# Graph layer and LSTM on one core: recurrent weights rounded in the graph's tail, low parts in 16 pieces, another order in the block loop

## The chip, the cores and the metric

The kernel runs on one core of one Trainium2 chip. The metric is the device time of one execution in microseconds. Three executions of the kernel before took 2735.42, 2737.44 and 2739.93 us; the median is 2737.44 us.

## The reference

A layer norm of x (6250 nodes, 512 features), a graph layer over 100000 edges sorted by destination, then a second layer norm and an LSTM over the 6250 rows as one sequence, each with a residual:

```python
agg = segment_sum(x[src], dst, 6250)            # x is the normalised input
h = relu((x + agg) @ W1 + b1)
x = x_in + relu(h @ W2 + b2)
# LSTM over the rows of layernorm(x), hidden size 512, f32
f, i, o = sigmoid([x_t, h] @ W_{f,i,o} + b); g = tanh([x_t, h] @ W_c + b_c)
c = f * c + i * g;  h = o * tanh(c);  y_t = x_t_in + h
```

## The kernel before

It has three stages with a barrier between them, each with a program of its own per engine and semaphores between these. Products are made in a rounded f32 type: each operand is split into a high part (rounded by ScalarE, `ACT.Copy`) and a low part (what is left, a subtraction), and two or three products are added.

**Table stage** (`table_part`, 0 to about 198 us). The rows of x are normalised and multiplied by W1; the result goes to DRAM as `ln_table`. GpSimd makes the low parts of W2 and of the LSTM's input weights here (L335, L339).

**Graph stage** (`graph_part`, to about 1402 us). 50 blocks of 125 nodes. Each block has 16 columns of 128 edges, and 7 blocks have one surplus column more. For each column GpSimd issues an indirect gather of 128 rows of 2 KB (L801) into a ring of 16 row buffers; it waits until VectorE has made the low part of the column that used the buffer before. ScalarE makes the high part (L836, 8 buffers), VectorE the low part (L994) and, four columns at a time, the one-hot matrix of destinations (L986); TensorE adds one-hot x high and one-hot x low to `agg` (L884). A surplus column is read after the 16 of its block: GpSimd waits for both consumers, loads the edges, waits for them, and gathers.

The loop is a software pipeline written out by hand: iteration i gathers block i, runs the layers of block i-1 and makes the LSTM's input products (`gps`, 48 matmuls, L904) of blocks i-1 and i-2. TensorE's order: turn `hin` (L898), columns 0 to 4, second layer `late` (12 products, L930 and L934), columns 5 to 7, gate products of banks 3 and 2, column 8, low gate products, columns 9 and 10, low products, turn z, columns 11 to 14, gate products, column 15, gate products. ScalarE's order: high parts 0 to 4, first layer (`first_layer`: relu of the turned rows, L848, and their high part, L853), high parts 5 to 13, the layer norm of z, high parts 14 and 15, high part of z. VectorE's: low parts 0 to 2, `hin`, one-hots, low parts 3 to 5, low part of h1 (L1038), `gate_biases` of banks 0 and 1 (L1015), one-hots 8 to 11, low parts 6 and 7, the layer's end and the statistics between low parts 8 to 11, then the rest. SyncE loads and stores the dense rows; it waits in the order of its list, and stores of the gates follow the biases.

The recurrent weights `Wh` lie in memory that the row buffers use too. One quarter is loaded in iteration 0; the rest by SyncE in iteration i = 50 (L780), before the last four gate stores.

**Recurrent stage** (`lstm_part`). 125 lanes of 50 steps run side by side: a rough round (38 steps, f16 intermediates, one product each), a "kept" round with high and low weights, and two rounds on changes. It begins with: GpSimd clears ten buffers (L1291 to L1294) and then subtracts four weight chunks of 2048 columns (L1301); ScalarE rounds two of the four chunks (L1353), VectorE the other two (L1729) after two casts of the identity (L1725, L1726); then VectorE casts the start state (L1732), and TensorE starts the first rough step with 4 products of the input rows (L1522) and 16 with the recurrent weights (L1491). A rough step has 13 VectorE operations on f16 with both inputs in SBUF, and 4 casts from PSUM. The low weights are needed in the kept round, some 200 us later.

Of the kernel before, what the change touches and what calls it, by code (L numbers as in the profile page):

```python
# [37 lines left out]
P = 128  # L38
# [17 lines left out]
def program(nc, x, src, dst, W1, b1, W2, b2, Wg, bg, y):  # L56
# [22 lines left out]
    with ExitStack() as top:  # L79
# [9 lines left out]
        ident = sb(top, "ident", [P, P])  # L89

# [17 lines left out]
        with ExitStack() as first:  # L108
# [14 lines left out]
            for half in range(2):  # L123
                for n, (bank, slot) in enumerate(((0, 0), (0, 1), (1, 0), (1, 1))):
# [4 lines left out]
            table_part(nc, x, src, dst, W1, W2, edges, table, loads, Wh, beside, Wx, W2s, s_wx, ident, ranges,  # L129
                       s_passed, sb, pb, sem, N, D, E, K, TILES, BLOCKS, TPP, TROWS)  # L130
            graph_part(nc, x, edges, table, x1_rows, gate_rows, Wx, W2s, b1c, b2r, bgr, s_w, 16 * (2 + 8),
                       Wh, beside, s_wh, gate_columns, ident, ranges,
                       s_passed, sb, pb, sem, D, E, K, BLOCKS, G4, HALF, PAIR)
        lstm_part(nc, x1_rows, gate_rows, total_rows, y, Wh, kept, s_wh, WH_LOADS, ident,
# [45 lines left out]
def table_part(nc, x, src, dst, W1, W2, edges, table, weight_loads, Wh, beside, Wx, W2s, s_wx, ident, ranges,  # L180
               s_passed, sb, pb, sem, N, D, E, K, TILES, BLOCKS, TPP, TROWS):
# [22 lines left out]
    with ExitStack() as ctx:  # L204
        held = sb(ctx, "held", [P, HELD, LB, D])

        def xin(n):
# [3 lines left out]
        W1p = Parts(*(sb(ctx, f"W1_{part}", [P, K, D], F32R) for part in ("high", "low")))  # L211
        xout = sb(ctx, "xout", [P, 2, LB, D])
        cT = [Parts(*(sb(ctx, f"cT{n}_{part}", [P, K, L], F32R) for part in ("high", "low"))) for n in range(2)]
# [20 lines left out]
        tile_i = sb(ctx, "tile_i", [BLOCKS, ETILE], I32)  # L234
        tile_f = (beside[0:BLOCKS, 3 * TPP * ETILE + TPP * BLOCKS:3 * TPP * ETILE + TPP * BLOCKS + ETILE]
                  .bitcast(F32))
        inside = sb(ctx, "inside", [BLOCKS, 1])
        row = sb(ctx, "row", [1, 6, BLOCKS])
        joints = sb(ctx, "joints", [1, 2, TROWS])
# [197 lines left out]
        def _(e):  # L437
# [121 lines left out]
            for k in range(K):  # L559
# [11 lines left out]
                      INSIDE_AT + 3: block_ranges}  # L571
# [14 lines left out]
def graph_part(nc, x, edges, table, x1_rows, gate_rows, Wx, W2s, b1c, b2r, bgr, s_w, WEIGHTS_LOADED,  # L586
               Wh, beside, s_wh, gate_columns, ident, ranges,
# [23 lines left out]
    with ExitStack() as ctx:  # L611
        node_id = sb(ctx, "node_id", [P, L])
# [9 lines left out]
        high = [sb(ctx, f"high{j}", [P, D], F32R) for j in range(PARTS)]  # L622
        low_part = [sb(ctx, f"low_part{j}", [P, D], F32R) for j in range(PARTS)]
# [31 lines left out]
        s_ends = sem(ctx, "s_ends_loaded")  # L655
        s_slab_x = sem(ctx, "s_slab_x")
# [82 lines left out]
        def _(e):  # L739
# [12 lines left out]
            def one(i, tiles, layers, gates):  # L752
# [77 lines left out]

        @block.scalar
        def _(e):
# [42 lines left out]
            all_iterations(e, one)  # L875

# [100 lines left out]
        def _(e):  # L977
# [40 lines left out]
            def one(i, tiles, layers, gates):  # L1018
# [25 lines left out]
                lows(6, 8)  # L1044
# [52 lines left out]
def lstm_part(nc, x1_rows, gate_rows, total_rows, y, Wh, kept, s_wh, WH_LOADS, ident,  # L1097
# [20 lines left out]
    with ExitStack() as ctx:  # L1118
        W_high = sb(ctx, "W_high", [P, K, 2, 2, 2, HALF], F32R)
        W_low = sb(ctx, "W_low", [P, K, 2, 2, 2, HALF], F32R)  # L1120
        ident_r = sb(ctx, "ident_r", [P, P], F32R)
        ident_h = sb(ctx, "ident_h", [P, P], F16)
# [66 lines left out]
        s_init_v = sem(ctx, "s_init_v")  # L1189
# [9 lines left out]
        BY_SCALAR = K // 2  # L1199
# [782 lines left out]
```

## Time and profile before

| | |
|---|---|
| profiled execution | 2735.91 us, its span 2734.0 us |
| median of three executions | 2737.44 us |
| TensorE matmul busy | 2516.1 us (92%) |
| VectorE busy | 2147.5 us (79%) |
| ScalarE busy | 1551.3 us (57%) |
| GpSimd busy | 1040.6 us (38%) |
| DMA | 611.09 MB, mean 224 GB/s |

Times in the profile are from the start of the span. Engine names: PE is TensorE, PEld its weight loads, DVE VectorE, ACT ScalarE, POOL GpSimd, SP SyncE; a q behind a name is the engine's sequencer. The ends of matmuls are modelled and overlap the next start, so distances between starts are the safer figure. "Idle" in square brackets is the engine's own idle time before the row, with what ended it.

### The profile page before, as it was taken

Reading aid. Unit: us, or ns where it says so; the run is one execution under the profiler, and the core shown is the slowest. Engines: PE = TensorE matmul, PEld = TensorE weight load, DVE = VectorE, ACT = ScalarE, POOL = GpSimd, SP = SyncE. Lnnn points to the kernel's source line nnn. Section 1 sums busy time; section 2 is a strip of 40 time slices with the busy share of each in tenths; the row PEclk is TensorE's granted clock in tenths of the full one; section 3 lists DMA queues with packets and bytes.
Section 4 is the critical chain, followed back from the end, with each engine's and each line's share of the span. In section 5 each row is a group of like instructions: output and inputs, shape, how many; then the busy total and the mean of one; then the engine's idle time right before and its main releaser. Section 6 shows DMA issues by size and latency. Waiting matters only on the chain. (4 is left out here: it accounts for less than half of the span.)

```text
span 2734.0 us, 47579 instructions
## 1 busy us (share of the span) xinstructions
PE 2516.1 (92%) x10762; PEld 1832.5 (67%) x10763; DVE 2147.5 (79%) x5752; ACT 1551.3 (57%) x3984; POOL 1040.6 (38%) x1010
## 2 busy tenths in 40 slices
PE   6986999999999999999959999999997999989996
PEld 4764777777777777777746666666665565555654
DVE  5846888888888888888858887777776777778886
ACT  4644555555555555555526655666664767757775
POOL 0307777777777767777630000000000000023332
PEclk9997999999999999999989999999998999999999
DMA  8547888888888878888857656777776666489995
GB/s 244 155 117 239 266 267 256 260 268 262 259 260 261 259 236 270 269 252 257 248 164 188 190 149 200 239 239 239 239 239 189 172 171 165 135 220 254 252 251 140
DMA packets 196506, 611.09 MB, mean 224 GB/s; under 512 B 41822, under 2 KB 51038, under 8 KB 166698
## 3 DMA queue, kind: packets, MB, share of 16 engines
q1 hardware_dynamic: 123632, 373.23, 45.4%
q0 software_dynamic: 72816, 237.24, 31.2%
q8 instruction: 18, 0.29, 0.0%
q14 instruction: 40, 0.33, 0.0%
HBM read 468.71 MB, written 141.62 MB: 223 GB/s over the span
## 5 line engine op out<-in xcount | busy, mean ns | idle before, releaser
L801 POOL DMA_INDIRECT kept<-ln_table,kept x800 | 856.7, 1071 | 341.8 <-issue 186.4
L1491 PE MATMUL acc<-W_high,state 128*125 128x512 f32 x3008 | 920.2, 410 | 62.5 <-DVE state L1789 47.2
L1491 PEld LDWEIGHTS acc<-W_high,state 128*125 128x125 f32 x3008 | 536.1, 186 | 233.2 <-ACT acc L1420 65.7
L994 DVE TENSOR_TENSOR low_part<-kept,high 128x512 fp32r<-128x512 f32 x800 | 523.3, 689 | 125.1 <-ACT high L836 119.3
L1326 POOL TENSOR_TENSOR out<-h,lx 125x512 f32<-125x512 f32 x50 | 64.7, 1293 | 1116.7 <-DVE h L1814 1116.7
L836 ACT ACTIVATE high<-kept 128x512 fp32r<-128x512 f32 x800 | 437.9, 629 | 80.8 <-DMA kept<-ln_table,kept 48.9
L884 PE MATMUL agg<-high,onehot 128*125 128x512 f32 x800 | 339.6, 424 | 45.9 <-DVE low_part L994 45.8
L884 PE MATMUL agg<-low_part,onehot 128*125 128x512 f32 x800 | 318.9, 399 | 0.0
L1491 PE MATMUL acc<-W_low,state 128*125 128x512 f32 x800 | 315.9, 395 | 0.0
L884 PEld LDWEIGHTS agg<-high,onehot 128*125 128x125 f32 x800 | 150.5, 188 | 119.7 <-DVE low_part L994 73.7
L904 PE MATMUL gps<-Wx_high,zT_high 128*125 128x512 f32 x800 | 219.2, 395 | 0.8 <-ACT zT_high L871 0.8
L904 PE MATMUL gps<-Wx_low,zT_high 128*125 128x512 f32 x800 | 218.1, 394 | 0.0
L904 PE MATMUL gps<-Wx_high,zT_low 128*125 128x512 f32 x800 | 209.3, 393 | 0.0
L1386 ACT ACTIVATE gate<-acc 125x512 f32<-125x512 f32 x200 | 119.7, 598 | 152.3 <-PE acc L1491 152.2
L1412 ACT ACTIVATE tc<-c 125x128 f32<-125x128 f32 x600 | 153.7, 303 | 90.1 <-DVE c L1806 89.7
L1796 DVE TENSOR_TENSOR c<-gate,c 125x256 f32<-125x256 f32 x300 | 126.4, 421 | 84.0 <-ACT gate L1386 82.1
L848 ACT ACTIVATE between<-hin_turned,b1c 128x125 f32<-128x125 f32 x200 | 56.6, 367 | 208.3 <-PE hin_turned L898 208.3
L904 PEld LDWEIGHTS gps<-Wx_high,zT_high 128*125 128x125 f32 x800 | 148.4, 186 | 38.2 <-issue 1.0
L904 PEld LDWEIGHTS gps<-Wx_low,zT_high 128*125 128x125 f32 x800 | 149.0, 186 | 37.3
L904 PEld LDWEIGHTS gps<-Wx_high,zT_low 128*125 128x125 f32 x800 | 147.8, 185 | 38.3
L884 PEld LDWEIGHTS agg<-low_part,onehot 128*125 128x125 f32 x800 | 151.3, 189 | 28.1
L1491 PEld LDWEIGHTS acc<-W_low,state 128*125 128x125 f32 x800 | 149.4, 187 | 30.3
(230 smaller groups left out, 4077.3 us busy)
## 6 DMA issues: line engine op xcount, KB each, us to landing
xg<-total_rows SPq DMA_DIRECT2D x100, 896.0 KB
xg<-gate_rows SPq DMA_DIRECT2D x88, 896.0 KB
gate_rows<-gout SPq DMA_DIRECT2D x200, 224.0 KB
total_rows<-total SPq DMA_DIRECT2D x50, 896.0 KB
kept<-ln_table,kept POOLq DMA_INDIRECT x800, 4.9
lx<-x_rows POOLq DMA_DIRECT2D x50, 250.0 KB, 7.5
out_dram<-out POOLq DMA_DIRECT2D x50, 250.0 KB, 3.0
held<-in_x_dram SPq DMA_DIRECT2D x25, 448.0 KB
```

Source lines behind the costliest of these rows:

```text
L801: e.indirect_dma_start(out=rows[j % RING][:, :], out_offset=None, in_=table[:, :], in_offset=bass.IndirectOffsetOnAxis(ap=ends[:, b, j, 0: ...
L836: e.activation(high[j % PARTS][:, :], rows[j % RING][:, :], ACT.Copy).then_inc(s_high, 1)
L848: e.activation(between_T[:, m, :], hin_turned[:, m, :], ACT.Relu, bias=b1c[:, m:m + 1]).then_inc(s_relu, 1)
L884: m = e.matmul(agg[0:L, :], onehot[:, j % HOT_RING, :], part[j % PARTS][:, :], start=(j == 0 and part is high), stop=(part is low_part), s ...
L904: products.append(e.matmul(gps[n][0:L, :], state[:, k, :], weights[:, k, n // 2, n % 2].rearrange("p s c -> p (s c)"), start=(begins and k ...
L994: e.tensor_tensor(low_part[j % PARTS][:, :], rows[j % RING][:, :], high[j % PARTS][:, :].bitcast(F32), ALU.subtract).then_inc(s_low, 1)
L1326: e.tensor_tensor(out[par][0:L, :], h[par][0:L].rearrange("c k u -> c (k u)"), x1[par][0:L, :], ALU.add).then_inc(s_out, 1)
L1386: e.activation(gates[0:L, half, 0].rearrange("c s u -> c (s u)"), sums, ACT.Sigmoid).then_inc(s_fi[half], 1)
L1412: e.activation(cell_turned[0:L, k], cell[0:L, k], ACT.Tanh).then_inc(s_tc[k], 1)
L1491: m = e.matmul(acc[n][0:L, :], stationary[:, k, :], weights[:, k, n // 2, n % 2].rearrange("p s c -> p (s c)"), start=begins, stop=(k == K ...
L1796: e.tensor_tensor(half_of(cell, half), gates[0:L, half, 0, 0].rearrange("c (k u) -> c k u", k=KH), half_of(cell, half), ALU.mult).then_inc ...
```

## The change

In the graph stage: ScalarE makes the high parts 5 to 7 ahead of the first layer, and VectorE the low parts 6 and 7 ahead of the gate biases of banks 0 and 1. The late load of three quarters of `Wh` moves from SyncE's iteration 50 to the end of GpSimd's program. Behind its last iteration ScalarE rounds these three quarters into `shared`, a buffer that in the table stage holds W1's parts and the turned rows, and in the graph stage the ring of high parts and four of the eight low parts.

In the recurrent stage: only the last quarter is rounded at the start, by ScalarE; VectorE rounds nothing. The identities are cast in the table stage. GpSimd clears the two buffers of the rough round first, signals these, clears the others, and then makes the low parts in 16 pieces of 512 columns; that they are there is waited for at the end of the rough round and no longer before a step. The first rough step begins from a zero state and makes no products with the weights: its input rows alone go to the gates.

```diff
@@ sync engine, graph stage
-                if isinstance(i, int) and i == BLOCKS:
-                    hold(e, s_passed, s_low, BLOCKS * COLUMNS + RING)
-                    hold(e, s_passed, s_hot, BLOCKS * COLUMNS // HOTS)
-                    for dst_ap, src_ap in gate_columns(Wh, D, (0, LAST)):
-                        e.dma_start(dst_ap, src_ap).then_inc(s_wh, 16)
@@ gpsimd, graph stage, behind its loop
+            e.wait_ge(s_low, BLOCKS * COLUMNS + RING)
+            e.wait_ge(s_hot, BLOCKS * COLUMNS // HOTS)
+            for to, of in gate_columns(Wh, D, (0, LAST)):
+                e.dma_start(to, of).then_inc(s_wh_rest, 16)
@@ scalar, graph stage
-                some(0, 5)
+                some(0, 8)
                 if layers:
                     first_layer(i)
-                some(5, 14)
+                some(8, 14)
...
             all_iterations(e, one)
+            e.wait_ge(s_wh, 16 * WH_LOADS // 2)
+            e.wait_ge(s_wh_rest, 16 * WH_LOADS // 2)
+            e.wait_ge(s_visit, BLOCKS * COLUMNS + COLUMNS)
+            for k in range(K - 1):
+                e.activation(shared[:, k * G4:(k + 1) * G4], Wh[:, k].rearrange("p a b s c -> p (a b s c)"), ACT.Copy)
@@ vector, graph stage
+                lows(6, 8)
                 if gates:
                     gate_biases(i - 2, 0)
                     gate_biases(i - 2, 1)
                 hots(8, 12)
-                lows(6, 8)
@@ vector, table stage, after block 20
+            def identities():
+                e.wait_ge(s_ids, 2)
+                e.tensor_copy(ident_r[:, :], ident[:, :])
+                e.tensor_copy(ident_h[:, :], ident[:, :])
@@ gpsimd, recurrent stage
-            for t in (c, c_start, h_start, gap, h_gap, change, r_c):
+            e.memset(r_c[:, :, :], 0.0).then_inc(s_clear, 1)
+            e.memset(r_decay[:, :, :], 1.0).then_inc(s_clear, 1)
+            for t in (c_start, h_start, gap, h_gap, change, tc_start, c):
                 e.memset(t[:, :, :], 0.0).then_inc(s_clear, 1)
-            for t in (decay, r_decay):
-                e.memset(t[:, :, :], 1.0).then_inc(s_clear, 1)
-            e.memset(tc_start[:, :, :], 0.0).then_inc(s_clear, 1)
-            e.wait_ge(s_wh, 16 * WH_LOADS)
-            for k in range(K):
-                if k < BY_SCALAR:
-                    e.wait_ge(s_init, 2 + k)
-                else:
-                    e.wait_ge(s_init_v, 3 + k - BY_SCALAR)
-                e.tensor_tensor(W_low[:, k].rearrange("p a b s c -> p (a b s c)"),
-                                Wh[:, k].rearrange("p a b s c -> p (a b s c)"),
-                                W_high[:, k].rearrange("p a b s c -> p (a b s c)").bitcast(F32),
+            e.memset(decay[:, :, :], 1.0).then_inc(s_clear, 1)
+            e.wait_ge(s_init, 1)
+            for n in range(LAST_PIECES):
+                at, to = slice(n * PAIR, (n + 1) * PAIR), slice((K - 1) * G4 + n * PAIR, (K - 1) * G4 + (n + 1) * PAIR)
+                e.tensor_tensor(W_low[:, to], Wh_flat[:, to], last_high[:, at].bitcast(F32),
+                                ALU.subtract).then_inc(s_clear, 1)
+            for n in range(PIECES):
+                at = slice(n * PAIR, (n + 1) * PAIR)
+                e.tensor_tensor(W_low[:, at], Wh_flat[:, at], shared[:, at].bitcast(F32),
                                 ALU.subtract).then_inc(s_clear, 1)
@@ scalar, recurrent stage
-            e.wait_ge(s_wh, 16 * WH_LOADS)
-            e.activation(W_high[:, 0:1, 0, 0, 0, 0:2], Wh[:, 0:1, 0, 0, 0, 0:2], ACT.Sigmoid).then_inc(s_init, 1)
-            e.wait_ge(s_init, 1)
-            for k in range(BY_SCALAR):
-                e.activation(W_high[:, k], Wh[:, k], ACT.Copy).then_inc(s_init, 1)
-            e.wait_ge(s_clear, CLEARED)
+            e.activation(gate[:, 0, 0, 0, 0:2], ident[:, 0:2], ACT.Sigmoid)
+            e.activation(last_high[:, :], Wh_flat[:, (K - 1) * G4:], ACT.Copy).then_inc(s_init, 1)
@@ tensor, recurrent stage, one_pass()
                         if first:
                             e.wait_ge(s_begin, r * 2 + 1)
                             for n in range(4):
                                 m = add_rows(n)
+                                if kind == "rough":
+                                    m.then_inc(s_acc[n], 1)
+                            if kind == "rough":
+                                e.drain().then_inc(s_taken, 1)
+                                e.wait_ge(s_init, 1)
+                                return
@@ vector, recurrent stage
-            e.tensor_copy(ident_r[:, :], ident[:, :]).then_inc(s_init_v, 1)
-            e.tensor_copy(ident_h[:, :], ident[:, :]).then_inc(s_init_v, 1)
-            e.wait_ge(s_wh, 16 * WH_LOADS)
-            for k in range(BY_SCALAR, K):
-                e.tensor_copy(W_high[:, k].rearrange("p a b s c -> p (a b s c)"),
-                              Wh[:, k].rearrange("p a b s c -> p (a b s c)")).then_inc(s_init_v, 1)
-            e.wait_ge(s_clear, CLEARED)
-            e.tensor_copy(state[:, :, :], h_start[:, :, :]).then_inc(s_begin, 1)
+            e.wait_ge(s_clear, 2)
+            e.sem_inc(s_begin, 1)
...
+                if kind == "rough":
+                    e.wait_ge(s_clear, CLEARED + PIECES + LAST_PIECES)
                 e.wait_ge(s_ends, r * 2 + 1)
```

Small buffers of the table stage and `node_id` also move into memory that is free at the time.

## Rows read from the trace of the kernel before

**Rows 1.** Stretch of the graph stage: us, then busy us (instructions) per engine, clock, DMA:

```profile
650.00:955.00 305.00, 298.19 (x1319) 233.00 (x1318) 258.88 (x514) 162.00 (x343) 230.12 (x211) 1.00 0.86 259
```

**Rows 2.** Order of time, TensorE: start us, us, engine, line, operation [idle before]:

```profile
707.59 0.40 PE L884 MATMUL agg<-high,onehot 128*125 128x512 f32 x1
...
709.92 1.10 PE L904 MATMUL gps<-Wx_high,zT_high 128*125 128x512 f32 x4
...
717.55 0.40 PE L884 MATMUL agg<-low_part,onehot 128*125 128x512 f32 x1
...
718.95 0.39 PE L884 MATMUL agg<-low_part,onehot 128*125 128x512 f32 x1
```

**Rows 3.** Order of time, ScalarE and VectorE in the same iteration:

```profile
702.69 1.13 ACT L848 ACTIVATE between<-hin_turned,b1c 128x125 f32<-128x125 f32 x4 [4.26 <-PE hin_turned L898]
704.30 4.80 ACT L836 ACTIVATE high<-kept 128x512 fp32r<-128x512 f32 x9
704.97 0.69 DVE L994 TENSOR_TENSOR low_part<-kept,high 128x512 fp32r<-128x512 f32 x1 [2.20 <-ACT high L836]
706.17 1.28 DVE L1015 TENSOR_TENSOR gout<-gps,bgr 125x512 f32<-125x512 f32 x2
708.02 1.28 DVE L994 TENSOR_TENSOR low_part<-kept,high 128x512 fp32r<-128x512 f32 x2
```

**Rows 4.** Order of time, GpSimd: the first gathers of blocks 19, 33, 37, 41, 47, 48:

```profile
630.90 0.95 POOL L801 DMA_INDIRECT kept<-ln_table,kept  x1 [0.30 <-issue]
955.07 0.95 POOL L801 DMA_INDIRECT kept<-ln_table,kept  x1 [0.30 <-issue]
1056.80 0.95 POOL L801 DMA_INDIRECT kept<-ln_table,kept  x1 [0.31 <-issue]
1144.35 0.95 POOL L801 DMA_INDIRECT kept<-ln_table,kept  x1 [0.30 <-issue]
1290.36 0.95 POOL L801 DMA_INDIRECT kept<-ln_table,kept  x1 [0.31 <-issue]
1319.07 1.11 POOL L801 DMA_INDIRECT kept<-ln_table,kept  x1 [0.31 <-issue]
```

**Rows 5.** The gather line's landing times, and a high part that waited for one:

```profile
DMA to landing us min/median/max: 3.4/4.9/7.4
...
1329.25 0.63 ACT L836 ACTIVATE high<-kept 128x512 fp32r<-128x512 f32 x1 [2.57 <-DMA kept<-ln_table,kept]
```

**Rows 6.** End of the graph stage: order of time, and SyncE's last wait:

```profile
1392.40 0.41 SPq L780 DMA_DIRECT2D kept<-in_L_ffn_W_f_dram  x1
...
1408.94 1.28 ACT L1350 ACT_TABLE_LOAD   x1 [19.79 <-PEq L611]
1410.47 3.71 ACT L1353 ACTIVATE W_high<-kept 128x2048 fp32r<-128x2048 f32 x2
...
SPq L793 <- DMA gate_rows<-gout: 4.8, 1, 4.8
```

**Rows 7.** Start of the recurrent stage: order of time, and a stretch with its clock:

```profile
1408.14 0.53 POOL L1291 MEMSET c<- 128x512 f32 x1 [45.31 <-POOLq L611]
1412.76 20.12 POOL L1301 TENSOR_TENSOR W_low<-kept,W_high 128x2048 fp32r<-128x2048 f32 x4
1423.74 4.71 DVE L1732 CAST state<-h_start 128x500 fp32r<-128x500 f32 x1
1433.69 0.29 DVE L1796 TENSOR_TENSOR total<-total 125x256 f16<-125x256 f16 x1 [5.25 <-ACT total L1386]
...
1428.00:1432.00 4.00, 3.34 (x8) 2.65 (x9) 0.45 (x1) 0.00 (x0) 4.00 (x2) 0.53 0.12 20
```

**Rows 8.** Table stage, order of time: GpSimd's subtractions and VectorE beside them:

```profile
65.45 5.04 POOL L335 TENSOR_TENSOR W_low<-W_stage,W_high 128x512 fp32r<-128x512 f32 x4
65.95 5.82 DVE L541 TENSOR_SCALAR ve<-mv 125x2 f32<-125x2 f32 x1
78.39 0.85 DVE L170 TENSOR_TENSOR rt<-rs 125x2 f32<-125x2 f32 x1
```

More of the change, by code:

```diff
@@ L177, in rsqrt_on_vector, with table_part @@
         last.then_inc(s_ready, 1)
-def table_part(nc, x, src, dst, W1, W2, edges, table, weight_loads, Wh, beside, Wx, W2s, s_wx, ident, ranges,
-               s_passed, sb, pb, sem, N, D, E, K, TILES, BLOCKS, TPP, TROWS):
+def table_part(nc, x, src, dst, W1, W2, edges, table, weight_loads, Wh, beside, Wx, W2s, s_wx, ident, ident_r, ident_h,
+               shared, ranges, s_passed, sb, pb, sem, N, D, E, K, TILES, BLOCKS, TPP, TROWS):
     LB = LOAD_BLOCKS
@@ L210, in table_part @@
         W_stage = sb(ctx, "W_stage", [P, K, D])
-        W1p = Parts(*(sb(ctx, f"W1_{part}", [P, K, D], F32R) for part in ("high", "low")))
+        W1p = Parts(*(shared[:, part * K * D:(part + 1) * K * D].rearrange("p (k d) -> p k d", k=K)
+                      for part in range(2)))
         xout = sb(ctx, "xout", [P, 2, LB, D])
-        cT = [Parts(*(sb(ctx, f"cT{n}_{part}", [P, K, L], F32R) for part in ("high", "low"))) for n in range(2)]
+        cT = [Parts(*(shared[:, (2 * K + 2 * n + part) * D:][:, 0:K * L].rearrange("p (k l) -> p k l", k=K)
+                      for part in range(2))) for n in range(2)]
         stats = sb(ctx, "stats", [P, 2, 6])
@@ L233, in table_part @@
         tile_no = sb(ctx, "tile_no", [BLOCKS, 1], I32)
-        tile_i = sb(ctx, "tile_i", [BLOCKS, ETILE], I32)
-        tile_f = (beside[0:BLOCKS, 3 * TPP * ETILE + TPP * BLOCKS:3 * TPP * ETILE + TPP * BLOCKS + ETILE]
-                  .bitcast(F32))
+        FREE = 3 * TPP * ETILE + TPP * BLOCKS
+        tile_f = beside[0:BLOCKS, FREE:FREE + ETILE].bitcast(F32)
+        tile_i = beside[0:BLOCKS, FREE + ETILE:FREE + 2 * ETILE]
         inside = sb(ctx, "inside", [BLOCKS, 1])
         row = sb(ctx, "row", [1, 6, BLOCKS])
-        joints = sb(ctx, "joints", [1, 2, TROWS])
+        joints = (beside[0:1, FREE + 2 * ETILE:FREE + 2 * ETILE + 2 * TROWS].bitcast(F32)
+                  .rearrange("o (two t) -> o two t", two=2))
         unsorted = sb(ctx, "unsorted", [1, 4])
@@ L570, in _ @@
                       BELOW_AT + 6: edges_inside, INSIDE_AT + 1: block_ends, INSIDE_AT + 2: columns_beyond,
-                      INSIDE_AT + 3: block_ranges}
+                      INSIDE_AT + 3: block_ranges, INSIDE_AT + 4: identities}
             for n in range(BLOCKS):
@@ L621, in graph_part @@
         rows += [later[:, j * D:(j + 1) * D] for j in range(LATER * G4 // D)]
-        high = [sb(ctx, f"high{j}", [P, D], F32R) for j in range(PARTS)]
-        low_part = [sb(ctx, f"low_part{j}", [P, D], F32R) for j in range(PARTS)]
+        node_id = beside[:, (RING - LATER * G4 // D) * D:][:, 0:L].bitcast(F32)
+        high = [shared[:, j * D:(j + 1) * D] for j in range(PARTS)]
+        IN_SHARED = (K - 1) * G4 // D - PARTS
+        low_part = [shared[:, (PARTS + j) * D:(PARTS + j + 1) * D] for j in range(IN_SHARED)]
+        low_part += [sb(ctx, f"low_part{j}", [P, D], F32R) for j in range(IN_SHARED, PARTS)]
         onehot = sb(ctx, "onehot", [P, HOT_RING, L], F32R)
@@ L1118, in lstm_part @@
     with ExitStack() as ctx:
[L1119 to L1122, printed above, removed]
+        last_high = sb(ctx, "last_high", [P, G4], F32R)
+        W_low = sb(ctx, "W_low", [P, K * G4], F32R)
+        W_high = [shared[:, k * G4:(k + 1) * G4] for k in range(K - 1)] + [last_high[:, :]]
         state = sb(ctx, "state", [P, K, L], F32R)
@@ L1480, in _ @@
                 e.sem_inc(s, DONE)
-            e.wait_ge(s_init, 1 + BY_SCALAR)
-            e.wait_ge(s_init_v, K - BY_SCALAR + 2)
             ROUNDED = [(state, W_high)]
-            OF_HIGH = [(state, W_high), (state, W_low)]
+            OF_HIGH = [(state, W_high), (state, [W_low[:, k * G4:(k + 1) * G4] for k in range(K)])]
             OF_LOW = [(h_low, W_high)]
@@ L1521, in add_rows @@
                         if kind == "rough":
-                            m = e.matmul(acc[n][0:L, :], ident_r[0:L, 0:L], rows, start=True, stop=False,
+                            m = e.matmul(acc[n][0:L, :], ident_r[0:L, 0:L], rows, start=True, stop=first,
                                          skip_group_check=True)
```

35 lines of the change are left out of this document (18 added, 17 removed).

## The prediction

> **What bounds the kernel now.** Read the busy table by stage first. In the graph stage (the loop over 50 blocks) TensorE is 98% busy at full clock and GpSimd, which only issues gathers, 75% (230.12 of 305) [rows 1]. That looks like a TensorE stage, but both figures mislead, so the order of time comes next, for TensorE, then for ScalarE and VectorE, and last the starts of GpSimd's gathers block by block.
>
> TensorE: from the first product of column 5 to the gate products behind column 7 are six products and 2.33 us; six starts of the same kind that wait for nothing (columns 11 to 14) take 1.40 us [rows 2]. So 0.93 us of each iteration is a wait for the low parts of columns 6 and 7, though the products' modelled ends hide it in the busy share. The other side explains it [rows 3]: ScalarE stands idle for 4.26 us until the turned rows come, does the first layer, and only then rounds column 5; VectorE waits 2.20 us for that, makes low part 5, then 1.28 us of gate biases, and only at 708.02 low parts 6 and 7.
>
> GpSimd: with the ring of 16 gathers full it is held back, and a block takes (955.07 - 630.90)/14 = 23.16 us, TensorE's own period. Where rows come late, a block takes (1144.35 - 1056.80)/4 = 21.89 us: its own pace. A block with a surplus column takes 28.71 us [rows 4]. Of the 49 intervals 14 are of the first kind, 28 of the second and 7 with a surplus column (they cost some 6.8 us more each). So GpSimd is 0.95 of a block's time in an ordinary iteration, and after each surplus column it is the one that the others wait for: ScalarE stood 2.57 us for a landing [rows 5].
>
> Between the stages TensorE has nothing to do for a while: the last stores drain 4.8 us [rows 6], then weights are rounded by ScalarE and VectorE while GpSimd holds VectorE up [rows 7].
>
> **Part 1: first layer behind eight columns, low parts 6 and 7 ahead of the gate biases.** Nothing is added; five instructions change places. Three roundings (4.80/9 = 0.53 us each, 1.6 in all) move into ScalarE's idle 4.26 us, if their rows are there: a gather lands 4.9 us after issue (3.4 to 7.4) [rows 5], and with the ring full row 7 is issued over 10 us before. VectorE can then do low parts 3 to 5 in a row, h1T_low at once, and 6 and 7 next, ready some 4.3 us after the turned rows begin, where TensorE wants them after 5.6 to 6.5. The biases move from 4.1 to 4.3 us, and SyncE's two stores behind them too: no one waits for either in the same iteration. TensorE's wait of 0.93 goes: 48 iterations (i = 2 to 49) x 0.93 = 44.6 us, if TensorE were all.
>
> It is not: what is late next is the gather. Made shorter by 0.93, the period is 22.2 us, still over GpSimd's 21.9, so the gathers no longer stand before a full ring, but seven surplus columns of 6.8 us (47.6 us) must fit, and the spare is 0.3 us a block instead of 1.3. Each surplus column after the first uses up the lead, and the stage then runs at GpSimd's sum. Before, that sum held 14 intervals x (23.16 - 21.89) = 17.8 us of waiting for a full ring; this is all that can be got. From it about 1.5 us go: eight rows must now have landed before the first layer, so after a surplus column the layer starts at about 9.6 (seven gathers of 1.37) + 4.9 - 0.6 = 14 us behind the block's first gather, where the iteration used to begin some 11 to 13 behind (column 3 of the block begun at 1319.07 came at 1329.25 and let the layer start then); this is paid once, at the last late block. In iteration 1, where rows come as they are gathered, the layer waits for about 4.5 us, of which most is covered, as ScalarE's square root stood behind column 13's landing anyway: 0.3 us. I take the graph stage at 16 us less (8 to 25: below, a gather slower by 0.01 us beside a denser VectorE costs 800 x 0.01 = 8; above, some of the lead outlives the surplus columns).
>
> **Part 2: recurrent weights loaded by GpSimd's queue at the end of its gathers.** The eight loads leave SyncE at 1392.40 and after [rows 6], where the last four gate stores stand behind them. They go to GpSimd, which has nothing left 22 us after its last block begins and is let go when the last low part is made, near 1370. The trace shows no such issue by GpSimd; its gathers are the nearest row, 1.25 us each with their gap, so 10 us, and twice that at most: landed between 1385 and 1395. ScalarE, idle 19.79 us from 1389.15 to 1408.94 [rows 6], now copies three quarters of the weights at 3.71/2 = 1.86 us each, 5.6 us. That ends by 1401 at the latest and hides under the last gate products; it would show only if the loads landed after 1401. The final drain of 4.8 us held traffic of those 3 MB, three times what the last gate stores move. It shrinks by something between 0 and 3; I take 2.
>
> **Part 3: start of the recurrent stage.** Removed from the path: identity casts, two roundings by VectorE, a cast of the start state that took 4.71 us for 500 elements, and 16 products of the first rough step. Before, the first vector operation of that step ran at 1433.69, which is 25.55 us after GpSimd's first memset at 1408.14 [rows 7]. On paper 18 us vanish, since rows and gates can be there some 8 us after that memset (an estimate: loads issued 1.3 us after it, a landing of 4.9 as a gather's, one gate). But GpSimd's 20 us of low parts stay, and VectorE's f16 operations have two inputs in SBUF. Rows show what that means: `rt<-rs` on two columns took 0.85 us, to the end of the GpSimd subtraction beside it (79.23); a tensor_scalar, also on two columns, behind five subtractions of 512 columns without a gap between them took 5.82, to the end of the last (71.7) [rows 8]. Behind pieces of 2048 columns a cast did get in at each border: it started at 1423.74 and took 4.71 [rows 7].
>
> If the 16 pieces act like the five, VectorE starts when GpSimd ends: 10 memsets (1412.76 - 1408.14 = 4.62) + 16 x 5.04/4 = 20.2, together 24.8, 0.7 earlier than before. Against it, TensorE has now nothing to do until then and meets the second step's products at the half clock, as it met the first step's: 0.53 in the first 4 us [rows 7]. That is at most 2 us, I take 1.5. Sum 0.8 slower. If a border lets one operation in, the 13 two-input operations of a step use up 13 borders, GpSimd ends 4 us later, and one step is done by then: about 2 us faster. I take 0 between them, with ends 18 faster and 2 slower.
>
> On this the Trainium skill's SBUF page ("SBUF — State Buffer", section on the two separate sides) says that a GpSimd operation and a VectorE operation with two SBUF inputs exclude each other for the whole instruction; the row with 0.85 us agrees. It says whoever is first has the pair, by which VectorE would get in at each border; the row with 5.82 us speaks against that for short pieces, and the row with 4.71 for it.
>
> The rounding of the identities in the table stage is two casts of 128 columns on a VectorE that waits for others there; 0, at most 1.3 for one wait behind a GpSimd subtraction (5.04/4) [rows 8]. Shared buffers change addresses only: 0.
>
> **Sum.** 16 + 2 + 0 = 18 us, from the profiled execution's 2735.91 us (span 2734.0): 2717.9. The median shown is 1.5 us above that execution, so the forecast of the median is 2719.4, say 2719.
>
> **Rivals.**
> (a) TensorE alone sets the graph stage: 44.6 + 2, about 2691. For it, 98% busy; against, the surplus columns and the landing wait.
> (b) VectorE slips between the pieces almost freely: it starts 8 us instead of 25.55 after the first memset, some 17 us earlier, so 35 in all: 2702. For it, the borders at 2048 columns; against, the 5.82 us.
> (c) Slower: three roundings in front of the first layer delay it in each iteration by 1.6 us, because rows are late or ScalarE's idle 4.26 is gone. Price: 1.6, less about 0.4 us by which its first product could start later at no cost, less the 0.93 saved, is 0.27, 48 times, 13 us net of the wait that goes: 2751. It decides where the lead of the gathers falls under 14 us in most iterations; only the seven surplus blocks and the first show that before.
> (d) Nothing in the graph stage: the wait only moves from columns 6 and 7 to `late` or hin, and only the drain is won: 2735. Against it, VectorE's hin was ready a microsecond before TensorE took it.
>
> **Chances.** Forecast (graph 10 to 25, start within 5) 0.62; (a) 0.08; (b) 0.14; (c) 0.05; (d) 0.08; the rest 0.03 between forecast and (d). What a measurement can tell from no change is 0.2%, 5.5 us. Faster by more: 0.88; within: 0.07; slower: 0.05. The range 2696 to 2732 takes in the bounds of the graph stage and most of (b), and leaves out (a) and (c).
>
> **What would show it.** The column 5 to gates distance falls to 1.4 us (wrong if over 2). Ordinary periods are 22.2 us, and GpSimd's blocks never 23.2; the sum of the 49 block intervals, 14 x 23.16 + 28 x 21.89 + 7 x 28.71 = 1138 before, falls to about 1121. ScalarE's waits for landings before column 5 to 7 appear behind surplus columns. The drain is about 3 us. The first f16 product of VectorE comes 24 to 26 us after the first memset of the recurrent stage (wrong, towards (b), if under 15). The forecast fails if GpSimd's ordinary block leaves 21.9 us, or if VectorE is not held.

## The result, and the profile after

| | before | changed |
|---|---|---|
| median of 5 runs, us | 2736.65 (2735.42 to 2739.93) | 2718.46 (2714.69 to 2724.78) |
| profiled execution: its own time, span | 2735.91, 2734.0 | 2714.69, 2712.9 |
| ratio of the medians | | 0.9932, 95% interval 0.9915 to 0.9949 |

Forecast 2719, measured 2718.46. The two profiled executions differ by 21.1 us of span, 3 more than the medians. The stretches below are cut at the first and last `hin_turned` products, GpSimd's first memset, the first gate of the rough round's third step, and the ends of the span:

| stretch, us | before | changed | difference |
|---|---|---|---|
| start to the first turned hidden block | 234.31 | 232.66 | -1.65 |
| graph stage, first to last turned block | 1142.96 | 1127.16 | -15.80 |
| last turned block to GpSimd's first memset | 30.87 | 27.62 | -3.25 |
| memset to the gate of step 3 | 35.46 | 33.03 | -2.43 |
| the rest | 1290.4 | 1292.4 | +2.0 |

The first and the last row lie within scatter and are not read as effects of the change: over all profiles of this case the first stretch varies from 231.1 to 236.5 us, on either kernel, and the last one by 6 us.

An ordinary iteration now, TensorE in order of time (start us, us, engine, line, operation, count, [idle before <- releaser]); column 5 and the gate products answer to [rows 2]:

```profile
696.65 0.39 PE L903 MATMUL agg<-shared,onehot 128*125 128x512 f32 x1
...
697.80 0.40 PE L903 MATMUL agg<-low_part,onehot 128*125 128x512 f32 x1
698.04 1.10 PE L923 MATMUL gps<-Wx_high,zT_high 128*125 128x512 f32 x4
```

ScalarE and VectorE in that iteration, as in [rows 3]:

```profile
691.72 1.13 ACT L862 ACTIVATE between<-hin_turned,b1c 128x125 f32<-128x125 f32 x4 [2.74 <-PE hin_turned L917]
693.33 2.20 ACT L850 ACTIVATE shared<-kept 128x512 fp32r<-128x512 f32 x4
694.09 1.29 DVE L1013 TENSOR_TENSOR low_part<-kept,shared 128x512 fp32r<-128x512 f32 x2
695.29 1.28 DVE L1034 TENSOR_TENSOR gout<-gps,bgr 125x512 f32<-125x512 f32 x2
```

Column 5 to the gates is 698.04 - 696.65 = 1.39 us instead of 2.33: the wait is gone. Low parts 6 and 7 are made at 694.09, ahead of the biases, 2.6 us before column 5's product. The same stretch as [rows 1] has TensorE busy all the time:

```profile
650.00:955.00 305.00, 305.00 (x1369) 244.10 (x1368) 272.67 (x537) 171.10 (x354) 238.11 (x220) 1.00 0.89 270
```

Period by period, from one `hin_turned` group to the next: the median falls from 23.21 to 22.29 us (0.91 before rounding), times 49 intervals 44.6 us. Call an iteration long when it is more than 0.5 us above the median, and add up what the long ones take above it: 4.6 us before, 32.5 now. Nine of the ten long iterations lie at and behind blocks with a column beyond sixteen (26.03, 23.79 + 23.27, 26.49 + 26.27, 23.44 + 23.59, 28.71 + 26.15); the tenth is the first of the stage, which was long before too. 44.6 - (32.5 - 4.6) = 16.7, the graph stage's gain within a microsecond. One such iteration in order of time, GpSimd, ScalarE, then TensorE:

```profile
968.72 1.35 POOL L823 DMA_INDIRECT rows_x<-ln_table,slab_x  x1 [4.37 <-DMA slab_x<-edges]
981.63 0.63 ACT L850 ACTIVATE shared<-kept 128x512 fp32r<-128x512 f32 x1 [2.24 <-DMA kept<-ln_table,kept]
984.75 1.12 ACT L862 ACTIVATE between<-hin_turned,b1c 128x125 f32<-128x125 f32 x4
...
981.37 0.59 PE L917 MATMUL hin_turned<-ident,hin 125*128 125x125 f32 x4
986.21 0.57 PE L949 MATMUL late<-W_high,h1T_high 128*125 128x512 f32 x1 [1.89 <-ACT h1T_high L867]
```

The stretch behind that stop, columns as in [rows 1]; then the longest stop of the stage and the stretch behind it:

```profile
986.00:990.00 4.00, 3.79 (x10) 2.96 (x11) 3.51 (x6) 3.44 (x7) 3.08 (x4) 0.57 0.80 242
...
445.61 0.49 PE L949 MATMUL late<-W_high,h1T_high 128*125 128x512 f32 x1 [3.44 <-ACT h1T_high L867]
...
445.60:449.60 4.00, 3.99 (x17) 3.25 (x18) 3.71 (x7) 2.96 (x6) 3.09 (x4) 1.00 0.69 191
```

GpSimd stands 4.37 us for the edge load. The next block's rows land late. ScalarE waits for the landings of five of its eight columns with the first layer queued behind them (2.24 us for one alone), so the layer starts 3.4 us behind the turned block (0.6 in the iteration above), and TensorE stops 1.89 us. Then its granted clock is 0.57 for 4 us, near the lower of its levels (1.2 of 2.4 GHz), and the same product starts 0.43 us after the last instead of 0.23: here the wait is paid nearly twice.

In the nine long iterations that is so behind three of TensorE's stops (986:990 at 0.57, 1013:1017 at 0.60, 1317:1321 at 0.57), and not behind the others: after the longest, 3.44 us, the clock is 1.00 and the products start 0.23 us apart. What decides between the two is open. The stops of more than 0.4 us in these iterations sum to 18 us; the three slow stretches cost some 5 us (an estimate: 3 x 4 x 0.42), so the waiting itself is the larger part of the price.

The tail and the start (ScalarE, GpSimd, VectorE):

```profile
1371.57 5.51 ACT L894 ACTIVATE shared<-kept 128x2048 fp32r<-128x2048 f32 x3
1387.44 0.52 POOL L1309 MEMSET total<- 128x512 f16 x1 [28.14 <-POOLq L622]
1392.07 4.92 POOL L1317 TENSOR_TENSOR W_low<-kept,last_high 128x512 fp32r<-128x512 f32 x4
1396.96 14.93 POOL L1321 TENSOR_TENSOR W_low<-kept,shared 128x512 fp32r<-128x512 f32 x12
...
1396.67 0.60 ACT L1400 ACTIVATE total<-acc 125x512 f16<-125x512 f32 x1 [5.15 <-issue]
1397.30 1.07 DVE L1806 TENSOR_TENSOR total<-total 125x256 f16<-125x256 f16 x1 [13.30 <-ACT total L1400]
1398.29 1.35 DVE L1811 TENSOR_TENSOR total<-total 125x256 f16<-125x256 f16 x1
1399.68 2.40 DVE L1816 TENSOR_TENSOR total<-total 125x128 f16<-125x128 f16 x2
```

The three roundings hide under the last gate products, as forecast. VectorE's first f16 operation comes 9.9 us behind the first memset (25.55 in [rows 7]), but each of them ends with one of GpSimd's pieces (1.2 us apart): it takes 1.07 to 1.37 us, where the same instruction takes 0.29 us alone. Step 1 lasts until GpSimd is done; the gate of step 2 comes at 1413.81.

### The profile page after: what moved, and what is told of

Read it like the earlier page. It is cut to its first block and busy times, and to the rows that moved or that the text cites. A ratio compares the mean times of both kernels' runs of the same rounds, so it can differ in the third digit from the quotient of the medians.

```text
span 2712.9 us, 47557 instructions
## 1 busy us (share of the span) xinstructions
PE 2510.2 (93%) x10746; PEld 1845.0 (68%) x10747; DVE 2149.1 (79%) x5749; ACT 1574.4 (58%) x3986; POOL 1037.9 (38%) x1030
## 5 line engine op out<-in xcount | busy, mean ns | idle before, releaser
L1503 PE MATMUL acc<-shared,state 128*125 128x512 f32 x2244 | 776.8, 416 | 63.3 <-DVE state L1799 47.2
L850 ACT ACTIVATE shared<-kept 128x512 fp32r<-128x512 f32 x800 | 458.2, 627 | 202.6 <-DMA kept<-ln_table,kept 149.8
L1503 PEld LDWEIGHTS acc<-shared,state 128*125 128x125 f32 x2244 | 402.0, 187 | 197.8 <-ACT acc L1434 66.0
L903 PE MATMUL agg<-shared,onehot 128*125 128x512 f32 x1200 | 378.3, 409 | 20.9 <-DVE shared L1013 17.3
L1503 PE MATMUL acc<-last_high,state 128*125 128x512 f32 x748 | 299.2, 400 | 0.0
L1013 DVE TENSOR_TENSOR shared<-kept,shared 128x512 fp32r<-128x512 f32 x400 | 268.7, 692 | 17.2 <-ACT shared L850 11.3
L903 PEld LDWEIGHTS agg<-shared,onehot 128*125 128x125 f32 x1200 | 217.4, 189 | 77.5 <-issue 19.0
L1013 DVE TENSOR_TENSOR low_part<-kept,shared 128x512 fp32r<-128x512 f32 x400 | 257.0, 692 | 8.1 <-ACT shared L850 8.0
L1005 DVE TENSOR_TENSOR onehot<-kept 128x500 fp32r<-128x500 f32 x200 | 135.4, 677 | 41.8 <-DVEq L1100 33.9
```

Of the source, the lines that this page charges most:

```text
L850: e.activation(high[j % PARTS][:, :], rows[j % RING][:, :], ACT.Copy).then_inc(s_high, 1)
L903: m = e.matmul(agg[0:L, :], onehot[:, j % HOT_RING, :], part[j % PARTS][:, :], start=(j == 0 and part is high), stop=(part is low_part), s ...
L1005: e.tensor_tensor(onehot[:, j % HOT_RING:j % HOT_RING + HOTS, :], node_id[:, :].rearrange("p (o l) -> p o l", o=1).to_broadcast([P, HOTS, L]),
L1013: e.tensor_tensor(low_part[j % PARTS][:, :], rows[j % RING][:, :], high[j % PARTS][:, :].bitcast(F32), ALU.subtract).then_inc(s_low, 1)
L1503: m = e.matmul(acc[n][0:L, :], stationary[:, k, :], weights[k][:, n * PAIR:(n + 1) * PAIR], start=begins, stop=(k == K - 1), skip_group_ch ...
```

## The experiments

Each median is of 4 to 11 executions, timed beside the kernel before (2735.9 to 2737.2 us there). Graph stage and start are those of the one profile of each kernel, as in the table above. The edits are shown shortened. Each kernel has, beside its own edit, that of the control, which moves a bound from where a number is loaded to where it is used:

```diff
-                min_val=0, max_val=E, ...
...
+                    before = nc.s_assert_within(before, 0, E)   # where a block has columns beyond sixteen
```

| kernel | median us | ratio, 95% interval | graph stage | memset to gate of step 3 |
|---|---|---|---|---|
| control | 2720.15 | 0.9939, 0.9922 to 0.9955 | 1129.15 | 32.60 |
| order undone | 2735.40 | 0.9995, 0.9986 to 1.0003 | 1147.25 | 32.01 |
| memsets for subtractions | 2709.09 | 0.9900, 0.9886 to 0.9913 | 1126.01 | 23.96 |
| four subtractions | 2720.78 | 0.9939, 0.9926 to 0.9951 | 1126.74 | 33.05 |
| spaced pieces | 2709.52 | 0.9899, 0.9884 to 0.9915 | 1130.94 | 22.91 |
| edge load ahead | 2692.82 | 0.9835, 0.9822 to 0.9849 | 1102.16 | 33.07 |
| four products fewer | 2691.26 | 0.9832, 0.9818 to 0.9845 | 1101.85 | 31.68 |
| seven columns | 2722.47 | 0.9951, 0.9937 to 0.9964 | 1129.74 | 31.36 |
| ScalarE's order on the kernel before | 2730.92 | 0.9981, 0.9972 to 0.9990 | 1132.95 | 36.96 |
| VectorE's order on the kernel before | 2706.19 | 0.9894, 0.9879 to 0.9909 | 1107.22 | 36.42 |
| edge load ahead, kernel before | 2740.86 | 1.0016, 1.0007 to 1.0025 | 1143.59 | 35.94 |
| spaced pieces + edge load ahead | 2684.48 | 0.9811, 0.9797 to 0.9824 | 1104.01 | 22.86 |

**Control.**

> The changed kernel with one more thing, that every experiment of this case has too: where an engine handles the columns beyond sixteen, the sequencer of ScalarE, TensorE, VectorE and GpSimd tests the number it loaded for them against its bounds once. That happens in the 9 or so blocks that have such columns. Every theory expects the changed kernel's time, 2718 us (2714 to 2724), ratio 0.993 to the kernel before; it is the control for the others.

2720.15 us: as expected within the spread. (The columns beyond sixteen lie in seven blocks.) Its rest behind step 3 took 1295.6 us, and 1294 to 1296.5 in every experiment, on either kernel, against 1290.4 before and 1292.4 changed. Why is open: the added test runs in the graph stage, whose two profiles differ by 2 us (1129.15 and 1127.16). So experiments are compared with the control and by stretches; those on the kernel before, which have no control, look up to 5 us worse than their edit is.

**Order undone.**

```diff
-                some(0, 8)
+                some(0, 5)
                 if layers: first_layer(i)
-                lows(6, 8)
                 if gates: gate_biases(i - 2, 0); gate_biases(i - 2, 1)
                 hots(8, 12)
+                lows(6, 8)
```

> The changed kernel with the first layer again behind five columns on ScalarE, and the last two low parts again behind the biases and one-hots on VectorE. Theory: the order alone made the 17.45 us by which the graph stage ends earlier; the time goes back to 2735 to 2738, the distance from column 5 to the gate products goes from 1.4 back to 2.3 us, ordinary iterations from 22.3 to 23.2, and the drain and the start keep their gain (the last turned hidden block to GpSimd's first memset 27.6 us, memset to the gate of step 3 33.0 us). Rival: the memory that the change moved about (high and low parts in the shared tile, loads issued by GpSimd) made the iteration shorter; then the time stays at 2718 to 2726.

2735.40, 15.3 us above the control; period 23.25 again, and the graph stage 18.1 us longer than the control's. The orders made the graph stage's gain, and the memory that was moved about made none (1147.25 against 1142.96 before). The other gains stay: the last turned block to the first memset takes 27.6 us here and in every kernel with the change but 26.6 with four products fewer, and 30.9 to 31.3 in the kernels without it.

**Each order alone, on the kernel before.** Of the diff above, ScalarE's two lines or VectorE's.

> The kernel before with ScalarE's order alone changed: the first layer behind eight columns instead of five; nothing else of the change. Theory: both orders are needed, since TensorE waited in each iteration for the low parts of columns 6 and 7, and these need the high part from ScalarE and then their place on VectorE, which stays behind biases and one-hots; less than a third of the 0.9 us per iteration is won, 2731 to 2737. Rival: ScalarE's order alone carries it (the high parts were what came late), ordinary iterations fall from 23.2 to 22.3 us and the time to 2719.

> The kernel before with VectorE's order alone changed: the low parts of columns 6 and 7 ahead of the biases and one-hots; ScalarE still has the first layer behind five columns. Theory (both orders are needed): the high parts of columns 6 and 7 still come behind the first layer, so VectorE now stands still for them with the biases and one-hots queued behind it; the iteration keeps its 23.2 us or gets up to 0.3 us longer, 2735 to 2752. Rival: VectorE's order alone carries it, 22.3 us and 2719.

Both theories fell, and both rivals had the period right. Either order alone brings it down (22.23 and 22.37), so TensorE's wait was for low parts 6 and 7, which need only one of two things: their high part earlier, or their place ahead of the biases. But ScalarE's order alone shortens the graph stage by 10.0 us and VectorE's by 35.7; long iterations hold 41.5 us in the one and 12.1 in the other. VectorE's order alone, 2706.19, is 12 us faster than the whole change (2718.46), without the gains of the drain and the start: ScalarE's order, once VectorE's is there, costs more than it brings. The iteration quoted above, with VectorE's order alone:

```profile
961.46 1.39 POOL L815 DMA_INDIRECT rows_x<-ln_table,slab_x  x1 [4.31 <-DMA slab_x<-edges]
981.66 1.13 ACT L850 ACTIVATE between<-hin_turned,b1c 128x125 f32<-128x125 f32 x4 [4.68 <-PE hin_turned L900]
983.77 0.39 PE L932 MATMUL late<-W_high,h1T_high 128*125 128x512 f32 x1
```

GpSimd stands as long for the edge load, but only five columns have to have landed before the first layer, ScalarE is ready 4.68 us early, and `late` waits for nothing. The waits tables of the stretch 300 to 1300 say it (us in total, times, longest), first with VectorE's order alone, where no wait of `late` is listed, then for the changed kernel:

```profile
ACT high L838 <- DMA kept<-ln_table,kept: 7.3, 10, 2.6
```

```profile
ACT shared L850 <- DMA kept<-ln_table,kept: 100.4, 112, 2.9
...
PE late L949 <- ACT h1T_high L867: 13.6, 8, 3.4
```

**Seven columns.** `some(0, 7)` ahead of the first layer; `lows(6, 7)`, bias, `lows(7, 8)`, bias on VectorE.

> The changed kernel with the first layer behind seven columns instead of eight on ScalarE, and on VectorE the seventh low part ahead of the biases, the eighth between them. Theory (after the blocks with columns beyond sixteen the lead of the gathers is too short for eight columns before the first layer; seven need 1.3 us less lead): the iterations after such blocks get 0.5 to 1.3 us shorter each, nothing else moves, 2 to 5 us in all, 2716. Rival (the column that is late there then delays the gate products, 2.33 against 1.4 us with five columns): 5 of 8 parts of the order's gain go and the time is 2720 to 2728.

2722.47 against 2720.15, intervals that overlap. The time lies in the rival's range, but neither mechanism is there: the ordinary period is 22.29, so the eighth column isn't needed early, and the long iterations hold 37.0 us, so one column less is too little. What five columns give is shown on the kernel before alone.

**Four products fewer.**

```diff
-                for k in range(K):
+                for k in range(1 if ends else 0, K):
```

> The changed kernel with 4 of the 48 gate products of each block left out (of the last low part of every bank the product of one chunk), so those parts of the gate sums are left out. It asks what bounds the ordinary iteration of 22.3 us now. Theory G, that of the prediction (GpSimd's gathers, 21.0 to 22.2 us per block, bound it or lie right behind): the 0.9 us of the four products give back 0.1 to 0.3 us per iteration, the graph stage gets 5 to 15 us shorter, 2705 to 2715. Rival T (TensorE alone bounds it, GpSimd stands before a full ring in most blocks): the whole 4 x 0.22 = 0.9 us in each of some 40 ordinary iterations, 35 us, 2685.

2691.26, 28.9 us less. The most frequent period goes from 22.29 to 21.29, the whole 4 x 0.25 us: TensorE alone bounds it, even one microsecond lower. GpSimd's blocks go down with it, to 21.29 too, though neither kernel shows it standing before a full ring in ordinary blocks (all its gaps are 0.30 us there; the kernel before stood 0.75 us longer per block): a missing stand is no sign that GpSimd sets the pace. The long iterations hold 57.1 us above 21.29 instead of the control's 34.4 above 22.29, which takes 23 of the 49 back. G, the prediction's theory, is refuted for the ordinary iteration.

**Edge load ahead, on both kernels.**

```diff
-                for j in range(COLUMNS):
+                for j in range(12):
                     gather(b * COLUMNS + j, b, j)
+                with e.If(extras[b % CHECKED] > 0):      # first column beyond sixteen
+                    gather_beyond(before, 0, begin)       # now only its edge load
+                for j in range(12, COLUMNS):
+                    gather(b * COLUMNS + j, b, j)
+                with e.If(extras[b % CHECKED] > 0):
+                    rows_beyond()
```

> The changed kernel with the edge load of a block's first column beyond sixteen issued behind the block's twelfth gather instead of behind its sixteenth, so that GpSimd does not stand still for its landing (3.4 to 4.9 us) before it issues the rows' gather. The blocks with such columns are the ones whose period is longer: 26.0, 23.8 + 23.3, 26.5 + 26.3, 23.4 + 23.6, 28.7 + 26.2 us instead of 22.3, together 27 us. Theory (in those blocks GpSimd's standing still is what the others wait for): of the 27 us 10 to 20 go, the time is 2700 to 2710. Rival (those blocks are long because TensorE has 3 products more and the gates and the first layer come late all the same): under 3 us, 2717 to 2720.

> The kernel before with only the edge load of a block's first column beyond sixteen issued behind the block's twelfth gather; the same edit took 27 us off the changed kernel. Theory (the ring's lead hid GpSimd's standing still while an iteration took 23.2 us, GpSimd needing 21 to 22, and no longer hides it at 22.3): the nine iterations behind such blocks took 23.6 us instead of 23.2 before, so there is only 0 to 5 us to win, 2732 to 2737. Rival (GpSimd's standing still is on the path with either order): 20 us or more, 2716.

On the changed kernel 27.3 us less than the control, more than expected; on the kernel before nothing (graph stage 1143.59 against 1142.96). GpSimd in the changed kernel with it, the load and then the rows' gather, in place of the 4.37 us above:

```profile
952.08 0.59 POOL L824 DMA_DIRECT2D slab_x<-edges  x1
960.08 1.11 POOL L828 DMA_INDIRECT rows_x<-ln_table,slab_x  x1 [0.30 <-issue]
```

Long iterations hold 6.4 us. The same stall cost nothing at 23.2 us per iteration and five columns, and 27 us at 22.3 and eight. VectorE's order alone tells which of the two matters: at 22.37 us and five columns the stall is still there (4.31 us above) and the iterations behind it are only 0.8 to 0.9 us above the median, the last 1.5. It is the eight columns ahead of the first layer that make it dear.

**Memsets for subtractions.**

```diff
-                e.tensor_tensor(W_low[:, to], Wh_flat[:, to], last_high[:, at].bitcast(F32), ALU.subtract)
+                e.memset(W_low[:, to].bitcast(F32), 0.0)
```

> The changed kernel with GpSimd's 16 subtractions replaced by 16 memsets of the same tile, so the low parts of the recurrent weights are left out (zero). It asks what it is in the subtractions that lets VectorE's two-input f16 operations in only once per piece (first step: 15.6 us from the first to the last of them). Theory P (two engines that both read two operands share one way into SBUF): a memset reads nothing, so VectorE's operations run in 0.2 to 0.6 us from the start, step 1 takes some 5.5 us from its first gate at 1396.7, the gate of step 2 comes about 16 us after GpSimd's first memset instead of 26.4, and the time falls by 9 to 11 us to about 2708. Rival M (any GpSimd instruction that streams holds VectorE until its end): memsets are shorter (0.5 us for 512 columns), 16 of them end 8 us after the ten others, so the gate of step 2 comes at 18 to 19 us, 7 to 8 us less, and single VectorE operations beside memsets show 0.5 us or more instead of 0.29.

The f16 operations beside the memsets (which run until 1397.54), and what came next:

```profile
1391.88 5.66 POOL L1322 MEMSET W_low<- 128x512 f32 x12
1395.45 0.29 DVE L1806 TENSOR_TENSOR total<-total 125x256 f16<-125x256 f16 x1 [13.47 <-ACT total L1400]
1395.72 0.29 DVE L1811 TENSOR_TENSOR total<-total 125x256 f16<-125x256 f16 x1
...
1398.47 1.21 PE L1534 MATMUL acc<-xg,ident_r 125*125 125x512 f32 x2 [2.46 <-DMA xg<-gate_rows]
```

Theory P: the same length as alone. That the gate of step 2 came at 18.7 us, M's number, has another cause: TensorE stood 2.46 us for the next rows. On this the Trainium skill ("SBUF — State Buffer", section on the two separate sides) says that a VectorE operation with two SBUF inputs is shut out only by a GpSimd operation that reads SBUF; 0.29 beside memsets and 1.07 to 1.35 beside subtractions agree.

**Four subtractions.** The same loop over 2048 columns.

> The changed kernel with the low parts in 4 subtractions of 2048 columns instead of 16 of 512. Theory B (one VectorE operation gets in at each border between two GpSimd instructions): with borders at 1397, 1402, 1407 and 1412 only three or four operations of step 1 are done when GpSimd ends, the rest (some 4 us) follow, so the gate of step 2 comes 30 us after GpSimd's first memset instead of 26.4, and the kernel is 2 to 4 us slower than the changed one: 2721. Rival (the two share the way evenly and the size of pieces is indifferent): the gate of step 2 stays at 26 to 27 us and the time at 2718.

```profile
1394.33 4.50 POOL L1319 TENSOR_TENSOR W_low<-kept,last_high 128x2048 fp32r<-128x2048 f32 x1
...
1399.13 4.32 DVE L1808 TENSOR_TENSOR total<-total 125x256 f16<-125x256 f16 x1 [12.86 <-ACT total L1402]
1403.37 4.58 DVE L1813 TENSOR_TENSOR total<-total 125x256 f16<-125x256 f16 x1
1407.99 4.54 DVE L1818 TENSOR_TENSOR total<-total 125x128 f16<-125x128 f16 x2
```

B as a mechanism is shown: one or two short operations per border, each ending with GpSimd's instruction. But the time is the control's: four take 18.0 us where 16 took 19.8, and step 3's gate stands at 33.05 against 32.60. Sixteen pieces bought a first step that ends with GpSimd, and moved that end back by 1.8: nothing on balance.

**Spaced pieces.**

```diff
-            for n in range(PIECES):                       # 12 of 512 columns
+            for n in range(PIECES):                       # 24 of 256 columns
+                e.wait_ge(s_decay, DONE + 1 + n)
```

> The changed kernel with the low parts of the first three chunks in 24 subtractions of 256 columns, each of them waiting for one more step of the rough round (behind VectorE's `decayed` of that step), instead of 12 of 512 in a row; the four of the last chunk stay. Nobody needs them before the rough round is measured. Theory (in the first step of the changed kernel VectorE waits for borders between GpSimd's subtractions): the gate of step 2 comes at 18 to 20 us after GpSimd's first memset instead of 26.4, as in the run with memsets in their place (18.7, bounded then by the rows' landing), and each of the 24 later pieces costs its step 0 to 0.3 us, since it is 0.6 us long and starts in VectorE's idle time; sum 4 to 9 us less than the control's 2720, so 2711 to 2716. Rival (each piece makes VectorE late by its own length in each of the 24 steps, 0.6 us each): 15 us lost in the round against 8 won, so 2727.

2709.52, 10.6 us less, a little better than expected. A piece, between VectorE's `decayed` and the next gates' products:

```profile
1414.57 0.73 POOL L1325 TENSOR_TENSOR W_low<-kept,shared 128x256 fp32r<-128x256 f32 x1 [4.62 <-DVE total L1833]
1415.37 0.29 DVE L1810 TENSOR_TENSOR total<-total 125x256 f16<-125x256 f16 x1 [0.28 <-ACT total L1404]
```

It holds up nobody: from step 3's first gate to the last gate of the rough round it takes 190.1 us, 190.3 in the control.

**Both winners.**

> The changed kernel with both edits that won: the edge load behind the twelfth gather (2692.8 alone) and the spaced subtractions (2709.5 alone, 10.6 less than the control's 2720.15). The one lies in the graph stage and the other in the recurrent stage. Theory (independent): 2692.8 - 10.6 = 2682, range 2678 to 2687. Rival (they share something, such as the clock granted after a graph stage with fewer pauses): 2690 or more.

2684.48, 1.9% below the kernel before and within 2.3 us of the sum. The runs point further, to VectorE's order with five columns on ScalarE, on top of these; that was not run.

## Why the prediction was right, step by step

- **The wait of 0.93 us goes, in 48 iterations.** Right: 0.91, in 49 intervals. Only VectorE's half of the two orders was needed for it.
- **"GpSimd's 21.9 us sets an ordinary block, and 14 intervals before a full ring are all that can be got; 16 us."** The size was right (15.8), the reason wrong. Ordinary iterations are TensorE's at 22.29, and would be at 21.29 (four products fewer). GpSimd's own pace isn't fixed: in blocks off TensorE's period it takes 20.4 to 22.4 us in the changed kernel, 20.98 twice in a row. The sum of its 49 block intervals fell to 1119.5 us, as announced (1121), but to 1101.6 with VectorE's order alone, where every surplus column still cost its stall; so 1120 was no floor. The forecast was to fail if GpSimd's ordinary block left 21.9 us: it did leave it, and the number held all the same. The trace before spoke against this step already: TensorE's period was at most 23.58 us in 47 of the 49 intervals, behind surplus columns too, so the 28 blocks of 21.89 were GpSimd making up its lead and not the pace of the stage. The loss of the changed kernel isn't spread over blocks but sits in nine iterations at and behind columns beyond sixteen.
- **"A lead of 14 us for eight columns, paid once, 1.5 us."** This is the term that was mis-sized. It is paid after each surplus column: the graph stage takes 1127.16 us with eight columns ahead of the first layer and 1107.22 with VectorE's order alone, 20 us (of which the moved memory could hold 4, the difference between the order undone and the kernel before). The price is TensorE's wait, 18 us in sum, and the half clock behind three of the stops, some 5 us, which the prediction did not think of here. This is the mechanism of rival (c), where (c) was said to decide, in the surplus blocks alone. The forecast's 17.8 - 1.8 and the measured 44.6 - 28 meet by chance: that is luck.
- **Rival (a), TensorE alone, 2691.** Against it stood the surplus columns. With either the edge load ahead or VectorE's order alone it comes to within 9 us of it in the graph stage (1102 and 1107 against 1143 - 44.6 = 1098): the bound in these blocks was the stall behind eight columns, not the number of gathers.
- **Drain 2 us.** 3.25, just above its upper end of 3.
- **Start 0, ends 18 faster and 2 slower.** 2.4 faster in the two profiles; 36 us before against 32 changed when all profiles are taken. The branch "a border lets one operation in, about 2 us faster" is what happened; the forecast took the middle between it and the five subtractions of [rows 8]. The announced sign, the first f16 operation at 24 to 26 us, was wrong (9.9), and would have pointed to rival (b); (b) is shown wrong with pieces in a row and right with spaced ones (10 us).
- **Roundings hidden, identities 0.** As forecast.

So the number was right through two opposite misjudgements inside one stage: an ordinary iteration that gives all it promised, and a rare one that takes most of it back.

## What to carry to other kernels

When an edit shortens the ordinary iteration, list the rare iterations too and ask of each what lead it lives on: a stall that cost nothing can become worth more than the edit, and moving it was worth 27 us here after being worth none. When two reorderings aim at one wait, price each alone; one was enough, and the other made the stage depend on late data. Work that nobody needs soon, and that shuts out another engine, belongs in that engine's gaps: spaced, the same subtractions were free.

## What the runs showed of the hardware

- GpSimd's subtractions in a row let VectorE's two-input operations in once per border (pieces of 512 columns: 1.07 to 1.37 us each; of 2048: 4.3 to 4.6), while a cast from PSUM beside them (`state<-hturn`, at 1407.01 in the changed kernel) took 0.28, its usual time. In [rows 8] a tensor_scalar stayed out over five such pieces; why is open. Sixteen pieces end 1.8 us later than four subtractions, some 0.15 us for each of the 12 borders more.
- A stop of TensorE of 1.89 us was followed by 4 us at a granted clock of 0.57, and products of 512 columns 0.43 us apart instead of 0.23. A stop of 3.44 us in the same stage was followed by 4 us at 1.00 and products 0.23 us apart: the length of the stop alone does not tell which of the two comes. What does is open.
- A product of 512 columns was worth 0.25 us of the period when four were left out; they start 0.23 us apart.
